# First expert blocks ahead of the gates' arithmetic in a two-layer transformer step

## What is computed

```python
def _L1_ffn_ref(x, W1, b1, W2, b2, Wr, br):          # x: layernormed, W1 (8, 256, 1024), W2 (8, 1024, 256)
    logits = x @ Wr + br
    idx = jnp.argmax(logits, axis=-1)
    probs = jax.nn.softmax(logits, axis=-1)
    gates = jnp.take_along_axis(probs, idx[..., None], axis=-1)[..., 0]
    for ei in range(e):
        h = jax.nn.gelu(xf @ W1[ei] + b1[ei], approximate=False)
        y = h @ W2[ei] + b2[ei]
        mask = (idxf == ei).astype(xf.dtype)
        out = out + y * (gf * mask)[:, None]
```

## Time and profile before

| | us |
|---|---|
| median of three executions | 423.94 |
| lowest and highest | 422.83, 426.74 |
| the profiled execution | 424.34 |
| its span | 422.4 |
| busy in the span: PE, DVE, ACT, POOL | 328.1, 242.4, 201.9, 192.0 |
| mean granted clock of TensorE | 0.873 of full speed |

### The profile page before, as it was taken

The page is one execution under the profiler, slowest core; times in us unless marked ns, Lnnn a source line. Parts: engine busy times, 40 slices in busy tenths (PEclk is TensorE's granted clock), DMA queues, the critical chain, the costliest instruction groups (busy, mean ns, idle before and its releaser), DMA issues.

```text
span 422.4 us, 8239 instructions
## 1 busy us (share of the span) xinstructions
PE 328.1 (78%) x2713; PEld 252.0 (60%) x2713; DVE 242.4 (57%) x561; ACT 201.9 (48%) x543; POOL 192.0 (45%) x244
## 2 busy tenths in 40 slices
PE   6727598698898897988988778463722999999993
PEld 2503475575666766767667465332421989899882
DVE  4444745469688887889888866735158123223220
ACT  2402586577595786867867466151110432423320
POOL 5321452484584865855847336281124023423322
PEclk9666889989899999999999899655555799999997
DMA  8880652726628737566366008981503011111111
GB/s 249 309 170 12 160 127 75 179 58 150 137 100 194 187 102 153 159 167 146 102 168 185 23 2 270 388 285 38 183 22 99 2 38 33 41 60 39 48 48 38
DMA packets 36694, 52.23 MB, mean 124 GB/s; under 512 B 10495, under 2 KB 28744, under 8 KB 36390
## 3 DMA queue, kind: packets, MB, share of 16 engines
q1 hardware_dynamic: 28716, 34.78, 31.9%
q10 hardware_dynamic: 6288, 12.33, 9.0%
q0 software_dynamic: 1648, 4.59, 3.5%
HBM read 42.81 MB, written 9.31 MB: 123 GB/s over the span
## 4 chain that ended last, share of the span: by engine, by line
PE 48%; DVE 21%; DMA 8%; issue 8%; POOL 8%; SPq 3%; ACT 3%; DVEq 0%; POOLq 0%; ACTq 0%
PE ps L590 46%; DVE mx L1719 5%; PE ps L594 2%; DVE W L1619 2%; DMA d_k<-W 2%; DMA W<-nmT 2%; DVE hold L1616 2%; DVE bst L1703 2%; POOL W L1484 2%; DVE W L1616 1%; DVE hold L1809 1%; SPq L517 1%; POOL W L1492 1%; POOL W L1463 1%; DMA W<-d_delta 1%
## 5 line engine op out<-in xcount | busy, mean ns | idle before, releaser
L590 PE MATMUL ps<-W 125*32 125x112 f32 (+2 forms) x1280 | 93.5, 271 | 29.6 <-DVE mx L1719 9.0
L590 PEld LDWEIGHTS ps<-W 125*32 125x32 f32 (+2 forms) x1280 | 64.1, 126 | 53.9 <-issue 21.6
L1719 DVE TENSOR_REDUCE mx<-ps 112x2 f32<-112x750 f32 x64 | 60.0, 938 | 42.3 <-PE ps L590 41.5
L1193 ACT ACTIVATE W<-ps 125x448 f32<-125x448 f32 x96 | 50.5, 546 | 37.0 <-PE ps L590 36.7
L590 PE MATMUL ps<-hold,proj 128*128 128x128 f32 (+2 forms) x288 | 52.5, 330 | 3.2 <-ACT W L1121 2.2
L1367 ACT ACTIVATE hold<-ps,consts 128x128 f32<-128x128 f32 x88 | 25.1, 367 | 51.1 <-PE ps L590 51.1
L590 PEld LDWEIGHTS ps<-hold,proj 128*128 128x128 f32 x288 | 39.4, 197 | 11.2 <-ACT W L1121 3.3
L1596 POOL DMA_INDIRECT out_x<-hold x11 | 16.3, 1478 | 63.7 <-DVE hold L1997 60.9
L590 PE MATMUL ps<-hold 128*128 128x128 f32 (+4 forms) x256 | 37.5, 300 | 8.2 <-DVE hold L1616 5.8
L594 PE MATMUL ps<-consts,hold 112*128 112x112 f32 (+3 forms) x136 | 27.5, 296 | 19.4 <-DMA hold<-d_x,hold 5.5
L590 PE MATMUL ps<-W,hold 128*128 x176 | 40.9, 386 | 0.0
(11 more groups left out here) (167 smaller groups left out, 552.4 us busy)
## 6 DMA issues: line engine op xcount, KB each, us to landing
W<-in_L_ffn_W SPq DMA_DIRECT2D x10, 1024.0 KB, 11.3
W<-in_L_ffn_W ACTq DMA_DIRECT2D x6, 1024.0 KB, 6.2
d_k<-W SPq DMA_DIRECT2D x16, 281.2 KB, 3.6
W<-d_k SPq DMA_DIRECT2D x16, 281.2 KB
hold<-in_ctxT SPq DMA_DIRECT2D x8, 375.0 KB, 4.0
W<-d_k SPq DMA_DIRECT2D x16, 187.5 KB
W<-d_q SPq DMA_DIRECT2D x48, 56.0 KB, 3.8
d_x<-hold ACTq DMA_DIRECT2D x8, 224.0 KB, 2.5
```

What stands on the lines that cost most here:

```text
L590: return pe.matmul(o, lhsT=l, rhs=r, start=start, stop=stop, skip_group_check=True)
L1193: act.activation(pexp[g % 2][0:LT, t, :], pE[n % 2][0:LT, 0:HG * T], ACT.Exp).then_inc(exp_done, 1)
L1719: dve.tensor_reduce(mx[:, 2 * i:2 * i + 2], pS[0:T, :, 0:L], X, ALU.max).then_inc(mx_done, 1)
```

## The change

One milestone more is counted: EBI, reached when the expert numbers `ebi` are written. ACT, POOL and DVE wait for it in place of SEL, and PE waits for it ahead of the block count. On DVE the three instructions of `outf` and `outi` go from ahead of the expert numbers to behind the gates' arithmetic. `sel` and `selx` go behind e_stage(0), and e_xT(0), e_stage(1), e_xT(1) go ahead of the gates' arithmetic. On PE the gates' matmuls go behind e_up(1) and e_xT(2), and e_xT(1) goes between the halves of e_up(0). `gcol` follows on DVE behind e_xT(2). In the earlier pipeline ACT's centre tap waits for another semaphore of DVE, `g_made` in place of `amc_ready`.

```diff
-    OH, LESS, LANES, ROWS, SEL, GATE = range(1, 7)
+    OH, LESS, LANES, ROWS, EBI, SEL, GATE = range(1, 8)
...
+            def e_gates():
+
+                pe.wait_ge(routed, GATE)
+                for b in range(B):
+                    last = mm(pZ[:, 64:64 + 3 * NB], inlane[:, b, :], share[:, b, :, :].rearrange("t c j -> t (c j)"), b == 0, b == B - 1)
+                last.then_inc(route_ps, 1)
+                pe.wait_ge(ebt_loaded, 16)
...
             e_xT(0)
-            pe.wait_ge(routed, GATE)
-            for b in range(B):
-                last = mm(pZ[:, 64:64 + 3 * NB], inlane[:, b, :], share[:, b, :, :].rearrange("t c j -> t (c j)"), b == 0, b == B - 1)
-            last.then_inc(route_ps, 1)
-            pe.wait_ge(ebt_loaded, 16)
+            pe.wait_ge(routed, EBI)
             pe.wait_ge(w_loaded, 16 * 2 * NE)
             total = blocks(pe)
-            e_up(0)
+            e_up(0, 0, M1 // 2)
             e_xT(1)
+            e_up(0, M1 // 2)
...
+                if j == 0:
+                    e_gates()
                 with filled_block(pe, total, j):
                     e_down(j)
...
                 if b >= 1:
-                    act.wait_ge(amc_ready, b)
+                    act.wait_ge(g_made, 2 * b - 1 + half)
...
-            step(ts(outf, rowf, 0.0, float(NT + 1), ALU.is_equal, ALU.mult))
-            step(dve.scalar_tensor_tensor(outf, rowf, -1.0, outf, ALU.add, ALU.add))
-            dve.tensor_copy(outi, outf)
...
-            dve.tensor_copy(ebi[:, :], ebj[0:1, :])
-            step(ts(sel, ebj[0:3 * NE, 0:NB], erow, None, ALU.is_equal, ALU.bypass))
-            dve.tensor_copy(selx, sel.unsqueeze(2).to_broadcast([3 * NE, NB, 128])).then_inc(routed, 1)
+            dve.tensor_copy(ebi[:, :], ebj[0:1, :]).then_inc(routed, 1)
...
-            dve.wait_ge(routed, SEL)
+            dve.wait_ge(routed, EBI)
             dve.wait_ge(w_loaded, 16 * 2 * NE)
             e_stage(0)
+            step(ts(sel, ebj[0:3 * NE, 0:NB], erow, None, ALU.is_equal, ALU.bypass))
+            dve.tensor_copy(selx, sel.unsqueeze(2).to_broadcast([3 * NE, NB, 128])).then_inc(routed, 1)
+            e_xT(0)
+            e_stage(1)
+            e_xT(1)
             dve.wait_ge(m_e, 1)
...
-            e_xT(0)
-            e_stage(1)
-            dve.wait_ge(route_ps, 3)
-            step(dve.tensor_copy(gcol, pZ[:, 64:64 + NB]))
-            step(tt(gcol, gcol, pZ[:, 64 + NB:64 + 2 * NB], ALU.add))
-            tt(gcol, gcol, pZ[:, 64 + 2 * NB:64 + 3 * NB], ALU.add)
-            e_xT(1)
+            step(ts(outf, rowf, 0.0, float(NT + 1), ALU.is_equal, ALU.mult))
+            step(dve.scalar_tensor_tensor(outf, rowf, -1.0, outf, ALU.add, ALU.add))
+            dve.tensor_copy(outi, outf)
```

More of the change, by code:

```diff
@@ L962, in e_xT, with e_up @@
                 last.then_inc(xT_ps, 1)
[L964 to L970, removed]
+            def e_up(j, lo=0, hi=M1):
+                if lo == 0:
+                    pe.wait_ge(xT_sb, j + 1)
+                    pe.wait_ge(w1_staged, j + 1)
+                    if j >= 2:
+                        pe.wait_ge(gelu_done, M1 * (j - 1))
+                for f in range(lo, hi):
                     o = ps[:, 2 * (j % 2) + f // 4, 128 * (f % 4):128 * (f % 4) + 128]
@@ L1356, in _ @@
             act.activation(m_e3, m_d3, ACT.Exp).then_inc(m_e, 1)
-            act.wait_ge(routed, SEL)
+            act.wait_ge(routed, EBI)
             total = blocks(act)
@@ L1590, in _ @@
                 e_rows(j)
-            pool.wait_ge(routed, SEL)
+            pool.wait_ge(routed, EBI)
             total = blocks(pool)
@@ L1990, in e_stage, with e_gates @@
                 dve.tensor_copy(w1st[j % 2], late[:, bass.ds(e * EW, DC * F1)]).then_inc(w1_staged, 1)
+            def e_gates():
+                dve.wait_ge(route_ps, 3)
+                step(dve.tensor_copy(gcol, pZ[:, 64:64 + NB]))
+                step(tt(gcol, gcol, pZ[:, 64 + NB:64 + 2 * NB], ALU.add))
+                step(tt(gcol, gcol, pZ[:, 64 + 2 * NB:64 + 3 * NB], ALU.add))
             def e_y(j):
```

## The result

The changed kernel takes 421.65 us against 425.67 for the kernel before (medians of 20 executions each, side by side). The ratio is 0.989, with a 95% interval of 0.9861 to 0.9919: 1.1% faster, 3.4 to 5.9 us. That ratio leaves out the slow executions (over 1.5% above the fastest of the same kernel: six of the changed kernel, three of the one before), and the two medians, which hold them all, differ by 0.9%. I had forecast 421.2 against 423.94, a gain of 2.7 us, 2.9 by the traces. Two more comparisons gave 0.993 and 0.989.

The account below looks back on a forecast made before the run. The serial DVE chain ahead of PE's run from e_up(1) was taken as what can move. Terms 0.70 + 1.93 + 0.51 − 0.24 = 2.90 us gave 421.44 or 421.04, forecast 421.2, range 419.9 to 423.1.

Parts of the forecast that it names:

- The bound: From e_up(1) on the chain is PE alone and stays untouched but for eight small matmuls; only its start can move.
- Page 0 earlier: POOL's first gather, with `selx` gone from beside it, takes about 0.97 us, so page 0's transposes start 0.7 us earlier.
- the first rival: DVE's weight copy holds POOL's first gather, so page 0 comes later; time about 422.8 us; chance 2 in 10.
- From page 0 to e_up(0): Start of page 0's transposes to start of e_up(0) shrinks from 3.24 to 1.31 us, a gain of 1.93.
- The stop ahead of e_up(1): With page 1's transposes inside e_up(0), PE's 0.74 us stop goes; transposes still take 0.23, gain 0.51 us.
- the near bound: TensorE's clock rises 3.5 us after e_up(0) starts instead of 5.9, a further gain of 1.1 us.
- Gates' matmuls: Eight matmuls on PE now between e_xT(2) and e_down(0), without waiting for GATE; a loss of 0.24 us.
- Edits at nothing: `outf`, third weight copy, ACT's table load and gelus, `gcol`, SP, POOL's wait and ACT's exchanged wait change no time.
- faster by over 1%: Whole kernel below 419.7 us, needing the clock's near bound and more; chance 0.06.
- The clock did not rise as late as before: Rival: TensorE's clock rises at 332.5 us as before, gain only 1.7, time 422.3 us; chance 1 in 10.
- PE did not stop inside e_up(0): Rival: page 1 lands late, PE idles inside e_up(0); 424.7 us for a 2 us stop; chance 1 in 20.
- the change did something: Rival denied here: page 0 no earlier and PE's register load longer than 0.62 us, time 423.9; chance 1 in 20.

Follow-up runs that it names:

- act_stage: Changed kernel with the first weight copy on ACT instead of DVE and `selx` behind page 0's copy; ratio 0.995 to the kernel before.
- gates_back: Changed kernel with the gates' arithmetic and matmuls ahead of e_up(0) again; ratio 0.997 to the kernel before.
- warm_before: Kernel before plus dummy matmuls on PE: 10 behind the counts, 20 behind the row numbers, 5 behind page 0's transposes; ratio 0.991 to the kernel before.
- no_split: Changed kernel with page 1's transposes behind the whole of e_up(0) on PE again; ratio 0.991 to the kernel before.
- wait_only: Kernel before with ACT's exchanged wait alone (`g_made` in place of `amc_ready`); ratio 0.998 to the kernel before.
- warm_long: Changed kernel plus dummy matmuls on PE, 10 behind the counts and 20 behind the row numbers; ratio 0.987 to the kernel before.
- warm: Changed kernel plus dummy matmuls on PE, 9 behind the counts and 10 behind the row numbers; ratio 0.987 to the kernel before.

## Why the prediction was right, and where a term was not

**The bound.** Right. From e_up(1) to the end of the span it took 88.4 us before and 88.3 after; everything was won ahead of it.

**Page 0 earlier (forecast 0.7): 0.41.** The mechanism held, since `selx` had stretched the first gather to 1.68 and its absence freed it. The length was mis-sized: I took 0.97 from the later gathers, and the first takes 1.21 here and in act_stage, with DVE's long copies away. The rest of the way to the transposes was 2.36 us, 2.29 before. The loss that the first rival foresaw, the weight copy holding page 0, did not come; the copy began 0.85 us into the gather, where I had it at 0.84.

**From page 0 to e_up(0) (forecast 1.93): 2.03.** Here I took PE's register load behind the transposes as the longer of two ways, 1.31 us. It was DVE's copy, 0.69 + 0.02 + 0.43 + 0.04, and 1.21 in all: PE waited 0.52 us for that copy, and the load lay beside it. gates_back puts 1.8 us of this on the gates' move.

**The stop ahead of e_up(1) (forecast 0.51) and the clock.** The stop is gone in every trace of the changed kernel. From the start of e_up(0) to e_up(1) it took 7.35 us before and 5.77 after, 1.58 less. The split gives 0.7 of it, as warm_before and no_split show (0.68 and 0.70), 0.17 more than my 0.51. The rest is the clock, which rose 1.9 us sooner after e_up(0) began: at 0.47 us for each us at the lower level, 0.9. This is the step in which the sum was too small: I held the rise at 5.9 us and named 3.5 as the near bound. The three profiles of the changed kernel gave 4.0, 6.1 and 3.4, from one end of that stretch to the other.

**Gates' matmuls (forecast a loss of 0.24): 0.10 lost.** From e_up(1) to e_down(0) it took 3.98 us before and 4.08 after. PE of the changed kernel:

```profile
332.40 3.74 PE L590 MATMUL ps<-hold,proj 128*128 128x128 f32 x32
335.97 0.38 PE L594 MATMUL ps<-consts,hold 128*128 128x128 f32 x2
336.19 0.36 PE L590 MATMUL ps<-hold 112*128 112x42 bf16 x8
336.48 0.28 PE L590 MATMUL ps<-w2T,w1T 24*128 24x256 bf16 x1
```

The eight matmuls push e_down(0) back by some 0.3 us. e_up(1) now follows e_up(0) with no idle time and takes 0.1 less to reach e_xT(2). GATE was there: no wait shows.

**Edits at nothing.** Right as far as the runs go: ACT's wait is 0.998 alone. The gelus and the `outf` instructions lie under PE's work.

**The total.** The sum was 2.90. The profile shows 4.1 from the row numbers on: −0.29, +0.10, +1.07, +0.14 for the four terms, and 0.2 behind e_down(0), where the transfer of the scatter before the last took 3.80 us instead of 4.06:

```profile
410.62 3.80 DMA out_x<-hold
412.09 4.06 DMA out_x<-hold
```

The first line is the changed kernel's chain, the second that of the kernel before. Without the clock's 0.9 the four terms come to 3.0, close to the 2.90: page 0's term was 0.29 too large, and the other three were too small, by 0.10 (page 0 to e_up(0)), 0.17 (the split) and 0.14 (the gates' matmuls). That they cancel to 0.1 is luck. There was luck in the time as well. The kernel before has a median of 425.67 us over 20 executions, 1.7 above the three-execution median that I subtracted from, and the gain was 4.0 instead of 2.7; the two errors nearly cancel, and 421.65 lies 0.45 from 421.2. The ratio itself, 1.1%, falls where I gave 0.06 (faster by over 1%), though its interval reaches to 0.8% and the medians say 0.9%.

Over three profiles the changed kernel reaches the end 99.9 us after its row numbers, against 103.8 for the old order (before and wait_only): 3.9 us. At a clock that is up in both, the order gives 3.1 to e_up(1) and 2.7 to 2.9 to the end. The three ratios, 0.989, 0.993 and 0.989, say 3 to 4.7 us. What is settled is the order's 3 us. That the clock rises sooner on average in the new order is not settled: five profiles with e_up(0) at 5.7 or 5.8 and no early warmth from dummies gave 2.8 to 6.1 and the two of the old order 5.7 and 5.9, but gates_back, with the old pattern ahead of e_up(0), gave 3.2.

**The other rivals.** The clock did not rise as late as before: behind the row numbers it rose at 9.7, 11.8 and 9.1 us in the three profiles, against 14.0 before. PE did not stop inside e_up(0) in any trace, and the change did something.

## What to carry to other kernels

When a serial stretch of small instructions ends in a long run of one engine, list what that run's first instruction really needs, and put everything else behind it: here the gates were needed only at the first scaling, and moving them won 1.8 of the 3 us. Compare such stretches from an event inside the program, not from the span's start: the part ahead scattered by 3.8 us, more than the change was worth. And look at the clock of the first matmuls behind a serial stretch; dummy matmuls in PE's idle time took the way from the row numbers to the end of the span from 99.9 us to 97.8, another 2.1.

## What the runs showed of the hardware

- TensorE's clock rose 3.4, 4.0 and 6.1 us after e_up(0) began in three executions of one kernel, and 2.8 to 5.9 us in the others without a warm start. A single trace's rise is a draw, and each us at the lower level costs 0.47 us here.
- With matmuls around them, it stayed up over idle times of 0.94 and 0.63 us ahead of and behind page 0's transposes (warm_long), and over 1.25 us ahead of them (warm_before), and fell 2.4 us after PE had stopped (warm). Twenty dummies of 512 columns took 4.48 us at the upper level.
- The first indirect gather took 1.21 us on POOL and the later ones 0.95 to 0.98, with no long copy of DVE in their first 0.6 us. Whether it is longer as the first one, or because POOL had been idle for 10.7 us, no run tells. One that met two long copies of DVE took 2.10.
- PE's register load of the block count, 0.62 us where nothing covers it, vanished beside a copy on DVE that PE waited for anyway.
